# Attention over a 32x32 image: the opening and the closing of the kernel rewritten

## The reference

```python
xr = x.reshape(B, C, S).transpose(0, 2, 1)
qkv = (xr @ w_qkv + b_qkv).reshape(B, S, N_HEADS, 3 * d_k)
q, k, v = jnp.split(qkv, 3, axis=-1)
attn = softmax(jnp.einsum('bihd,bjhd->bijh', q, k) * scale, axis=2)
out = jnp.einsum('bijh,bjhd->bihd', attn, v).reshape(B, S, N_HEADS * d_k)
out = out @ w_proj + b_proj
return out.transpose(0, 2, 1).reshape(B, C, H, W) + x
```

## Time and profile before

| | |
|---|---|
| median of 3 runs | 4039.3 us |
| the profiled execution, its own time | 4035.91 us |
| its span (first to last instruction) | 4034.1 us |
| granted TensorE clock, mean of the span | 0.996 |
| PE busy | 3933.0 us, 97% |
| DVE / POOL / ACT busy | 82% / 75% / 73% |
| first score tile of unit 0 starts | 87.42 us |
| last value product ends, output projection follows | 3983.6 us |

### The profile page before, as it was taken

The page is one execution under the profiler, slowest core; times in us unless marked ns, Lnnn a source line. Parts: engine busy times, 40 slices in busy tenths (PEclk is TensorE's granted clock), DMA queues, the critical chain, the costliest instruction groups (busy, mean ns, idle before and its releaser), DMA issues.

```text
span 4034.1 us, 60038 instructions
## 1 busy us (share of the span) xinstructions
PE 3933.0 (97%) x18464; PEld 3355.3 (83%) x18464; DVE 3309.2 (82%) x4442; ACT 2934.7 (73%) x5527; POOL 3008.7 (75%) x2376
## 2 busy tenths in 40 slices
PE   4999999999999999999999999999999999999997
PEld 3878888888888888888888888888888888888885
DVE  3888888888888888888888888888888888888884
ACT  2777777777777777777777777777777777777774
POOL 1787777787777877777777777877778777777775
PEclk9999999999999999999999999999999999999999
DMA  6343443444334444443444434443344444434432
GB/s 185 86 121 106 120 110 106 112 117 127 102 102 114 111 125 115 117 105 100 130 108 118 112 105 112 118 129 100 101 116 111 125 114 113 108 99 130 109 86 71
DMA packets 263375, 453.33 MB, mean 112 GB/s; under 512 B 107920, under 2 KB 118160, under 8 KB 258960
## 3 DMA queue, kind: packets, MB, share of 16 engines
q1 hardware_dynamic: 263056, 449.48, 42.1%
HBM read 206.58 MB, written 41.42 MB: 61 GB/s over the span
## 4 chain that ended last, share of the span: by engine, by line
PE 88%; issue 4%; DVE 3%; ACT 3%; POOL 1%; SPq 1%; DMA 1%; ACTq 0%; POOLq 0%; DVEq 0%
PE ps_g L397 24%; PE s L419 10%; PE ps_o L533 10%; PE ps_o L531 10%; PE st L473 10%; PE st L471 10%; PE ps_g L413 9%; DVE acc L655 2%; PE st L518 1%; PE st L519 1%; ACT p_hl L595 1%; ACT x_h L550 1%; ACT p L592 1%; POOL p_hl L760 1%; DVE stage L734 0%
## 5 line engine op out<-in xcount | busy, mean ns | idle before, releaser
L760 POOL TENSOR_TENSOR p_hl<-p,p_hl 128x512 fp32r<-128x512 f32 x2048 | 2603.7, 1292 | 934.5 <-ACT p_hl L595 933.6
L592 ACT ACTIVATE p<-st 128x512 f32<-128x512 f32 x2048 | 1232.5, 602 | 711.5 <-PE st L473 700.1
L658 DVE TENSOR_REDUCE nm<-s 128x1 fp32r<-128x1024 f32 x1024 | 1250.6, 1221 | 370.2 <-PE s L419 359.3
L655 DVE TENSOR_TENSOR acc<-acc,p 128x512 f32<-128x512 f32 x1792 | 1236.3, 690 | 26.2 <-ACT p_hl L595 0.5
L595 ACT ACTIVATE p_hl<-st 128x512 fp32r<-128x512 f32 x2048 | 1240.8, 606 | 0.0
L531 PE MATMUL ps_o<-p_hl,v_hl 128*128 128x512 f32 x2048 | 801.5, 391 | 4.3 <-POOL p_hl L760 3.6
L473 PE MATMUL st<-q,k 128*128 128x512 f32 x2048 | 803.4, 392 | 0.0
L533 PE MATMUL ps_o<-p_hl,v_hl 128*128 128x512 f32 x2048 | 800.4, 391 | 0.0
L471 PE MATMUL st<-q,k 128*128 128x512 f32 x2048 | 798.3, 390 | 0.4 <-DMA q<-max_d 0.4
L397 PE MATMUL ps_g<-x_h,wq 128*128 128x512 f32 x2016 | 711.6, 393 | 6.6 <-DVE qk_l L636 6.6
L419 PE MATMUL s<-k,q 128*128 128x512 f32 x2048 | 646.4, 396 | 9.4 <-DVE nm L658 9.4
(11 more groups left out here) (78 smaller groups left out, 3699.5 us busy)
## 6 DMA issues: line engine op xcount, KB each, us to landing
wq<-wq_d SPq DMA_DIRECT2D x128, 512.0 KB, 4.5
k<-qk_h SPq DMA_DIRECT2D x256, 256.0 KB, 4.2
wv<-wv_d SPq DMA_DIRECT2D x32, 1024.0 KB, 5.5
q<-qk_h SPq DMA_DIRECT2D x128, 256.0 KB, 3.8
q<-qk_l SPq DMA_DIRECT2D x128, 256.0 KB, 4.9
k<-qk_l SPq DMA_DIRECT2D x128, 256.0 KB, 5.1
q<-q SPq DMA_DIRECT2D x256, 128.0 KB, 4.9
rinv<-rinv_d SPq DMA_DIRECT2D x256, 128.0 KB, 2.8
```

Source lines behind the costliest of these rows:

```text
L592: nc.scalar.activation(p[:, to, :], st[slot % RING][:], ACT.Exp)
L655: nc.vector.tensor_tensor(acc[:], acc[:], probs, ALU.add).then_inc(acc_done, 1)
L658: nc.vector.tensor_reduce(nm[:, it:it + 1], s1[:], AXX, ALU.max, negate=True).then_inc(max_done, 1)
L760: nc.gpsimd.tensor_tensor(p_l[:, to, :], p[:, to, :], p_h[:, to, :].bitcast(f32), ALU.subtract).then_inc(pl_done, 1)
```

## The change

The middle of the kernel stays as it is. At the opening, SP issues all loads without a store among them; only block 3 waits (for block 0's place, L310). Each weight block has a split place of its own, lent by buffers that are not yet in use. PE makes q and k of heads 0 and 1 block by block straight from these places (four banks side by side, L530) and four value groups from the split value weights (`first_v`, L489), the last three between the first passes. The split weights still go to DRAM, for all later heads: those of q and k in four pairs of DMAs (`store_wqk`, L316) around `move_head(0)`, those of the values in eight DMAs in unit 3 (`store_wv`, L321). The output weights are loaded in unit 9, split in units 13 to 16, and the bias sums stand in unit 14 (`BIAS_SUM`).

At the closing the extra turn is gone. The attention output of heads 0 to 5 of the last image is split in units 48 to 58 (`OS_LAST`, ACT and DVE) into the places of `x`, which no further image needs; the residuals are loaded ahead, each into a buffer of its own (`RES_LAST`, `res_last`). After the last sums PE makes four output tiles over three of the four channel blocks (36 matmuls), then their last block (12), then the same for the other four, each tile in its own bank (`out_banks`).

```diff
--- before.py
+++ after.py
...
+    OS_LAST = {48: (0, 0), 49: (1, 0), 50: (0, 1), 51: (1, 1), 54: (0, 2), 58: (1, 2)}
+    RES_LAST = {48 + g: g for g in range(XRING)} | {57: XRING, 58: XRING + 1}
...
+    WP_SPLIT = {13 + k: k for k in range(KT)}
+    BIAS_SUM, BIAS_ADD = 14, 16
...
-        v_banks = [ps_g, st[2], ps_o]
+        v_banks = [ps_g, st[2], ps_o, acc]
+        out_banks = [ps_g[:], st[1][:], st[2][:], s1[:, cols(0)], s1[:, cols(1)], ps_o[:], acc[:], st[0][:]]
+        res_last = [t[:] for t in ring] + [t[:] for t in stage] + [p[:, i, :] for i in range(2)]
...
+            def store_wqk(k):
+                sp.wait_ge(wqk_low, QK_PARTS * (k + 1))
                 for s in range(2):
...
+                    sp.dma_start(wq_d[:, :, s, k, :].rearrange("h p c -> p h c"), qk_split[k][:, s].bitcast(f32)
+                                 ).then_inc(wqk_stored[k], 16)
...
+            def store_wv(k):
+                for s in range(2):
+                    sp.dma_start(wv_d[:, :, s, k, :].rearrange("a p (h d) -> p a h d", h=4),
+                                 v_split[k][:, s].rearrange("p (a h) d -> p a h d", a=2).bitcast(f32)
+                                 ).then_inc(wv_stored, 16)
...
             for k in range(KT):
-                if k >= 2:
-                    sp.wait_ge(w_low, W_PARTS * (k - 1))
-                sp.dma_start(w_stage[k], w_qkv[k * P:(k + 1) * P, :].rearrange("p (h c) -> p h c", h=HEADS)
-                             ).then_inc(w_loaded[k], 16)
+                if k < KT - 1:
+                    load_w(k)
                 for c in (k, k + KT):
                     sp.dma_start(x_stage[c], x_chunk(0, c)).then_inc(x_staged[c], 16)
-                if k >= 2:
-                    store_w(k - 2)
+            sp.wait_ge(wqk_low, QK_PARTS)
+            sp.wait_ge(wv_low, V_PARTS)
+            load_w(KT - 1)
...
-            for k in (2, 3):
-                sp.wait_ge(w_low, W_PARTS * (k + 1))
-                store_w(k)
-            sp.dma_start(wp_stage, w_proj.rearrange("(k p) n -> p k n", p=P)).then_inc(wp_loaded, 16)
-            for i in range(2):
-                sp.wait_ge(w_stored[i], 16 * 4 * 2)
-            load_wq(0)
-            load_wq(1)
-            load_wv(0)
+            store_wqk(0)
             sp.wait_ge(l_done, 2)
             move_head(0)
-            sp.wait_ge(qk_done, 2)
-            load_wq(2)
+            store_wqk(1)
             sp.wait_ge(moved[0], 16 * MOVES)
             fill_q2(0, 0)
+            store_wqk(2)
+            store_wqk(3)
             sp.wait_ge(max_done, 4)
             store_max(0)
             sp.wait_ge(max_stored[0], 16)
             load_max(0)
+            for k in range(KT):
+                sp.wait_ge(wqk_stored[k], 16 * 2)
+            load_wq(2)
...
+                    if U == 3 and B.first:
+                        sp.wait_ge(wv_low, V_PARTS * 3)
+                        sp.wait_ge(wv_last, V_PARTS)
+                        for k in range(KT):
+                            store_wv(k)
...
+                    if U == (8 if B.first else 4):
+                        if B.first:
+                            sp.wait_ge(wv_stored, 16 * 2 * KT)
                         sp.wait_ge(v_done, at(8, 4))
                         load_wv(1)
+                    if U == 9 and B.first:
+                        sp.dma_start(wp_stage, w_proj.rearrange("(k p) n -> p k n", p=P)).then_inc(wp_loaded, 16)
...
+                    if U in RES_LAST and B.final:
+                        g = RES_LAST[U]
+                        if g < XRING:
+                            for i in range(2):
...
+                        load_res_last(g)
 
             bodies(body)
+            sp.wait_ge(recip_done, HALVES * BATCH - 1)
+            store_inverse(0)
+            sp.wait_ge(recip_stored[0], 16 * HEADS * BATCH)
+            load_inverse(HALVES - 2)
+            sp.wait_ge(st_free, SLOTS * BATCH + 1)
+            store_sums(HALVES - 1)
+            sp.wait_ge(row_stored[1], 16 * HEADS * BATCH)
+            load_sums(1)
+            sp.wait_ge(pl_done, 2 * UNITS * BATCH - 2)
+            sp.wait_ge(acc_done, 2 * UNITS * BATCH - 2)
+            for g in (6, 7):
+                load_res_last(g)
+            sp.wait_ge(recip_done, HALVES * BATCH)
+            store_inverse(1)
+            sp.wait_ge(recip_stored[1], 16 * HEADS * BATCH)
+            load_inverse(HALVES - 1)
+            for g in range(8):
+                sp.wait_ge(out_ready, 8 * (BATCH - 1) + g + 1)
+                sp.dma_start(tile_of(out, BATCH - 1, g), res_last[g]).then_inc(stored[g % 2], 16)
...
+            for k in range(KT):
+                pe.wait_ge(x_low[k // 2], NH * (k % 2 + 1))
+                pe.wait_ge(wqk_low, QK_PARTS * (k + 1))
+                for i in range(QK0):
+                    for e in range(k * NT // KT, (k + 1) * NT // KT):
+                        _, part, j = TERMS[e]
+                        mm = nc.tensor.matmul(qk_banks[i][:], qk_split[k][:, part, i // 2, :], xs[j][:, k, cols(i % 2)],
+                                              start=e == 0, stop=e == NT - 1)
+                    if k == KT - 1:
+                        mm.then_inc(qk_done, 1)
+            pe.wait_ge(wv_low, V_PARTS * 3)
+            pe.wait_ge(wv_last, V_PARTS)
+            for tile in range(2):
+                mm = first_v(0, tile)
+            mm.then_inc(v_done, 1)
             pe.wait_ge(moved[0], 16 * MOVES)
-            pe.wait_ge(bias_done, 2)
             for it in range(MAX0):
                 if it:
                     pe.wait_ge(max_done, it)
                 first_scores(0, it).then_inc(s1_done, 1)
+                pair, tile = 1 + it // 2, it % 2
+                if pair > 1:
+                    pe.wait_ge(l_done, pair - 1)
+                mm = first_v(pair, tile)
+                if tile == 1:
+                    mm.then_inc(v_done, 1)
             pe.wait_ge(l_done, QK0)
-            pe.wait_ge(vl_done, V0)
+            pe.wait_ge(vl_done, 2)
             pe.wait_ge(ready, 1)
...
+                    if U == BIAS_SUM and B.first:
+                        pe.wait_ge(l_done, held[1] + 1)
+                        pe.wait_ge(wp_loaded, 16)
+                        pe.wait_ge(const_loaded, 16 * 4)
+                        for m in range(KT):
+                            for k in range(KT):
+                                mm = nc.tensor.matmul(ps_g[:, m:m + 1], wp_stage[:, k, m * P:(m + 1) * P], bv[:, k:k + 1],
+                                                      start=k == 0, stop=k == KT - 1)
+                        mm.then_inc(bias_summed, 1)
+                        held = ("bias", 0)
+                    if U == 1 and B.first:
+                        pe.wait_ge(vl_done, V0)
...
             bodies(body)
+            last = Body(BATCH)
+            weighted_values(last, -1)
+            pe.wait_ge(st_free, SLOTS * BATCH - 2)
+            sums(st[0], HALVES * BATCH)
+            done = range(0, NT - NT // KT), range(NT - NT // KT, NT)
+            pe.wait_ge(out_ready, 8 * (BATCH - 1))
+            for n in range(NH):
+                pe.wait_ge(last_low, 5 + n)
+                for part in range(2):
+                    if part == 1:
+                        pe.wait_ge(last_low, 7 + n)
+                    for g in range(KT * n, KT * n + KT):
+                        if part == 0 and g == 1:
+                            pe.wait_ge(st_free, SLOTS * BATCH)
+                        if part == 0 and g == 3:
+                            pe.wait_ge(max_done, UNITS * BATCH)
+                        if part == 0 and g == 5:
+                            pe.wait_ge(half_done, HALVES * BATCH)
+                        if part == 0 and g == 7:
+                            pe.wait_ge(st_free, SLOTS * BATCH + 1)
+                        mm = product(out_banks[g], lambda i, k: wp[i][:, k, g % KT * P:(g % KT + 1) * P],
+                                     lambda j, k: xs[j][:, k, cols(n)], done[part])
+                        if part == 1:
+                            mm.then_inc(prod_done, 1)
...
+            w_low_qk(0)
+            w_low_v(0)
+            w_low_qk(1)
+            w_low_qk(2)
+            w_low_v(1)
+            w_low_qk(3)
+            dve.wait_ge(const_loaded, 16 * 4)
+            nc.vector.tensor_scalar(bqk[0:D, :], bqk[0:D, :], SCALE, None, ALU.mult).then_inc(bias_done, 1)
+            dve.wait_ge(bias_done, 1)
+            for i in range(2):
+                dve.wait_ge(h_done, i + 1)
+                qk_low(0, i, qk_banks[i])
+            w_low_v(2)
             for i in range(2):
                 nc.vector.memset(k2[i][0:1, :].bitcast(f32), 1.0).then_inc(ready, 1)
...
             for it in range(MAX0):
-                dve.wait_ge(s1_done, it + 2)
+                if it == 4:
+                    for i in range(2):
+                        dve.wait_ge(h_done, i + 3)
+                        qk_low(1, i, qk_banks[i + 2])
+                dve.wait_ge(s1_done, it + 1)
...
```

(51 more changed lines are left out.)

372 lines of the change are left out of this document (204 added, 168 removed).

## The result

The changed kernel takes 3988.3 us (median of four runs, 3987.35 to 3990.56), the kernel before 4038.9 in the same comparison: a ratio of 0.9875, 95% interval 0.9864 to 0.9887. The forecast was 3985.0, with a range of 3975 to 3998. So it is faster, and by less than forecast: by the two profiled spans, 4034.1 and 3985.9, 48.2 us against the 54.3 of the sum. (By the medians it is 50.6, because the median of before lies 3 us above its profiled run and that of after 0.3 above its own.) So the sum is some 6 us too large, and the question is which terms were.

What follows compares the result with a forecast made beforehand. PE bounds the middle (busy 239.15 of 240 us), so gain lies only at the ends, where engines wait: opening -32.4, closing -21.9, together -54.3 us, giving 3981.6; 3.4 for the median makes 3985.0, range 3975 to 3998.

Steps and rivals of the forecast that it cites:

- Steps 1 to 4: Opening: block 3 landed at 17.5, split by 21.9; head 0's moves issued at 25.0, ended at 33.0 us.
- Step 5: Opening: queue of stores empty at 45.5, then the row of maxima; first score tile at 49.3 instead of 87.42 us.
- The sentence on the Trainium skill's 358 GB/s: Opening: at that rate stores take 8.8 us, queue empty by 42.3, forecast 2.7 us lower; not adopted.
- rival C: Opening and extra splits: less waiting than charged, stores at 429 GB/s taking 7.3 us, not 12.0; 3977; chance 0.13.
- Step 6: Opening, units 0 to 2: head 1's moves land in time; unit 2 starts at 54.8, 40.5 us earlier.
- Step 7: Around unit 14: bias sums cost 3.5 us, the low clock behind them 1.6, output-weight splits 1.0.
- Step 8: Queue in units 3 to 12: loads in units 8 and 9 make a row late; 2.0 us (0 to 5.8).
- The closing's main part: After the last sums: 96 output matmuls in 22.1 us if splits are in time; end at 4010.2, -23.9 us.
- The splits of the last image: Units 48 to 58: six more ACT copies and six DVE subtractions cost 2.0 us, at most 4.2.
- A: Opening: stores hold SP, the eight value stores cost 3 us each; some 11 us go back; 3996; chance 0.17.
- B: Closing: DVE gives all of 4.2 us to the last units, last splits 3 us late; 3990; chance 0.07.
- D: From unit 14: granted clock stays low after the bias sums; whole gain gone, time passes 4039.3; chance 0.03.

Runs made afterwards that it cites:

- e3: Changed kernel with the last image's six low halves of units 48 to 58 made on POOL instead of DVE; 3983.5 us.
- e5: Changed kernel with the opening reordered: head 1's moves ahead of the last store of split weights, two value lows between the maxima; no time given, first score tile at 48.74.
- e10: Changed kernel without the last image's six low halves of units 48 to 58, ACT's copies kept; no time given, 0.2 us given back there.
- e1: Changed kernel without the bias sums, the output-weight splits kept; no time given, 2.9 us given back in units 14 to 19.
- e2: Changed kernel with the bias sums spread, one column in each of units 14 to 17; 3980.5 us.
- e4: Changed kernel with the last image's six low halves kept on DVE but one input read from PSUM; 3984.8 us.
- e8: Changed kernel with bias sums spread over units 14 to 17 and output-weight splits moved to units 19, 23, 27 and 31; 3983.5 us.
- e13: As e8, but each low half of the output weights one unit after its high half; 3981.5 us.

## Why the prediction was right or wrong, step by step

- Steps 1 to 4 held to 0.2 us: the splits done at 21.8, moves issued at 25.14 (25.0), landed at 33.09 (33.0). The products of blocks 0 to 2 and the bias vectors ahead of DVE's low parts cost nothing, as said.
- Step 5 had the right time, 48.93 for 49.3, by luck, for the reason was wrong. The queue was through at about 42.8, not 45.5: the windows from 33 to 43 add up to 3.0 MB at 301 GB/s, where I had put 3.15 MB in 12 us (262). The sentence on the Trainium skill's 358 GB/s (page "DMA: Bandwidth & Descriptors", section "Where 436 GB/s comes from") gave 42.3, nearer than mine, though its rate was not reached: some 0.3 MB of the stores had moved before 33 us. (By the prediction's own terms 42.3 makes the forecast 3.2 us lower, not 2.7, and in rival C 49.3 becomes 45.8, not 46.2.) The row of maxima was issued 2.5 us before the 45.5, and that was lost again: PE's own value products last until 47.80, and then PE waits 1.13 us for something that the prediction did not list, the low halves of the value groups, behind the sixth maximum on DVE.
- Step 6 held: unit 2 at 54.06 (54.8). Head 1's moves, called in time, came 0.57 us late for PE; from unit 4 on the lead is 40.2 for 40.5.
- Step 7, the clock after the bias sums, was mis-sized: 8.8 us in the profiled run (6.7 to 8.8 over the seven kernels), 6.1 charged. The mechanism, low clock behind the sums, was named, and the 3.5 us for the sums held in e3, e5 and e10 (3.73), where the clock stayed up to their end; in after it fell during them (4.98). Too small above all were the splits, put at 1.0: e1 shows 2.9 with the sums gone.
- Step 8 was too high: 0.5 us in after for units 3 to 14 (at most 1.5 in the other kernels), 2.0 charged. (Its 360 GB/s of step 1 is 371 there, 3.15 MB in 8.5 us.)
- Between unit 19 of the first image and unit 48 of the last 0.4 us are given back, for which nothing was charged.
- The closing's main part held: 23.3 us for 23.9. The output products have no gap, as forecast. The low clock at the change to output tiles, which was not charged, takes 1.6; with the clock at 1.00 (e1, e2, e4, e5) it is 24.9, more than forecast.
- The splits of the last image are the step that failed: 5.6 us for 2.0, over the 4.2 that I had called the most. I charged 0.7 for each and let waits hide half of it. DVE has next to none in units 50 to 57 (busy for 30.06 of 32 us), so nothing was hidden (e4: 4.8, where six at 0.69 make 4.1), and the waits for POOL add 0.8. The trace of before had a row on this very form, the low halves of `x`, which I had not read:

```profile
L721 DVE TENSOR_TENSOR x_l<-ring,x_h x60: 690/892/1837, 256.0 to 3705.6; 128x512 fp32r<-128x512 f32 x60
```

Its longest is 1.84 us; six at up to that would have put the bound at 11, not at 4.2.

Together: 2.7 (step 7) + 3.6 (splits) + 0.6 (closing) + 0.4 (the middle) + 0.3 (step 6) - 1.5 (step 8) = 6.1, the difference between 54.3 and 48.2. By luck the median of before lay 2.7 us higher above its profiled run than that of after, which hid nearly half of it.

Of the rivals, A did not occur (SP was held for 3.46 us by two stores and nobody waited; the eight value stores took 0.8 us each to issue, from 57.02 to 63.33), C was right in that stores go faster than charged, but gained nothing by it. B's first half came true, at 5.6 in place of 4.2 us; its second half, late last splits, did not. D's beginning is there (0.50 after the sums), its end is not: the clock is back at 1.00 after some 6 us.

## What to carry to other kernels

Price an added instruction by the engine that sets the pace in that very stretch: six copies on ACT cost 0.2 us and six subtractions on DVE 5.4 in the same units. In an engine's fixed order a wait costs what stands behind it, so the second half of a two-engine step belongs a unit behind the first (e8 to e13: 2.6 to 0.9 us). One-column products on TensorE are put between full matmuls, not in one stretch (e2: 2.6 us given back, the splits' share included, for 6.7 to 8.8).

## What had not been expected of the hardware

A DVE subtraction of two SBUF operands took 0.69 to 1.84 us for one and the same form (60 in before), by what POOL did at its start; an addition of the same size with an operand in PSUM 0.678 to 0.700 us in 1792 cases. And in all seven kernels that have 32 one-column matmuls in a row the granted clock fell from 1.00 to 0.50, in four while they ran (3.95 to 5.14 us for the 32), in three up to 1.3 us after; in the four kernels with four parts of eight between full matmuls it stayed at 1.00, and the parts cost 1.3 us where nothing else stood beside them (e8).
